# Second attention: the column of x with the key bias as a row sum on VectorE and ScalarE, instead of one-column products on TensorE

## The reference

```python
q = jnp.einsum('bld,de->ble', query_states, Wq) + bq
k = jnp.einsum('bld,de->ble', key_states, Wk) + bk
v = jnp.einsum('bld,de->ble', value_states, Wv) + bv
scores = jnp.einsum('bqd,bkd->bqk', q, k) / math.sqrt(HEAD_SIZE)
scores = scores + (1.0 - attention_mask)[:, None, :] * -10000.0
probs = jax.nn.softmax(scores, axis=-1)
context = jnp.einsum('bqk,bkd->bqd', probs, v)
```

## Time and profile before

| | us |
|---|---|
| median of 3 runs (377.69 to 378.69) | 377.79 |
| profiled execution, its own time | 375.65 |
| span of its instructions | 373.9 |
| TensorE busy | 354.1 |
| VectorE busy | 182.5 |
| ScalarE busy | 149.7 |
| GpSimd busy | 57.6 |

### The profile page before, as it was taken

One profiled execution on the slowest core, in us unless ns is written; L12 is line 12 of the kernel. 1 busy time (PEld: TensorE's weight loads), 2 busy tenths in 40 slices (PEclk: granted clock), 3 DMA queues, 4 the chain that ended last, 5 costly groups with the idle time before them and its releaser, 6 DMA issues.

```text
span 373.9 us, 7935 instructions
## 1 busy us (share of the span) xinstructions
PE 354.1 (95%) x3108; PEld 266.4 (71%) x3108; DVE 182.5 (49%) x573; ACT 149.7 (40%) x361; POOL 57.6 (15%) x95
## 2 busy tenths in 40 slices
PE   3889999999999999998889999999889999999996
PEld 2446666766657665755668998998768889797875
DVE  4964345647566465564462122212489667532500
ACT  0524553554454553535533221120345667523300
POOL 2730000010101000010120000030694421200000
PEclk9999999999999999999999999999999999999999
DMA  8946060603400100000207499970110011111000
GB/s 245 351 111 227 0 225 3 220 20 96 144 1 15 28 4 13 2 15 2 70 12 213 136 334 335 303 210 25 50 50 1 3 53 52 40 39 50 26 25 25
DMA packets 24885, 35.29 MB, mean 94 GB/s; under 512 B 2608, under 2 KB 21408, under 8 KB 24736
## 3 DMA queue, kind: packets, MB, share of 16 engines
q1 hardware_dynamic: 22160, 31.73, 26.9%
q0 software_dynamic: 768, 1.84, 1.7%
q10 hardware_dynamic: 1920, 1.21, 1.2%
HBM read 31.06 MB, written 3.72 MB: 93 GB/s over the span
## 4 chain that ended last, share of the span: by engine, by line
PE 85%; DVE 6%; DMA 5%; issue 2%; ACT 1%; POOL 0%; SPq 0%; DVEq 0%; ACTq 0%; POOLq 0%
PE ps L417 10%; PE ps L575 8%; PE ps L720 8%; PE ps L585 7%; PE ps L431 7%; PE ps L698 6%; PE ps L454 6%; PE ps L385 6%; PE ps L361 5%; PE ps L651 3%; PE ps L352 3%; DMA xres<-in_x 2%; PE ps L667 2%; PE ps L477 2%; PE ps L521 2%
## 5 line engine op out<-in xcount | busy, mean ns | idle before, releaser
L1056 DVE TENSOR_REDUCE mneg<-ps 112x2 f32<-112x750 f32 x64 | 57.1, 933 | 42.3 <-PE ps L417 41.9
L833 ACT ACTIVATE heads<-ps 125x896 f32<-125x896 f32 x48 | 41.4, 915 | 17.5 <-PE ps L437 17.5
L1273 POOL TENSOR_TENSOR rstd<-veps,neghalf 112x1 f32<-112x1 f32 x32 | 18.5, 577 | 194.1 <-DVE veps L1022 193.9
L417 PE MATMUL ps<-heads 32*112 32x375 f32 x256 | 38.5, 518 | 1.8 <-DVE mneg L1056 1.4
L431 PE MATMUL ps<-heads 32*125 32x224 f32 x384 | 32.2, 374 | 0.7 <-DVE mneg L1056 0.6
L361 PE MATMUL ps<-ctxT,w_in 128*128 128x375 f32 x64 | 25.6, 524 | 7.3 <-DMA ctxT<-in_ctxT 5.9
L575 PEld LDWEIGHTS ps<-xT,ring 128*128 128x128 f32 x256 | 29.8, 192 | 1.1 <-ACT xT L788 0.7
L575 PE MATMUL ps<-xT,ring 128*128 128x112 f32 x256 | 29.9, 275 | 0.4 <-ACT xT L788 0.4
L720 PE MATMUL ps<-heads,ring 128*112 128x256 f32 x128 | 28.8, 382 | 0.0
L585 PE MATMUL ps<-ring,heads 128*112 128x256 f32 x128 | 28.8, 379 | 0.0
L454 PEld LDWEIGHTS ps<-heads,vones 125*17 125x17 f32 x768 | 17.2, 97 | 13.9 <-issue 12.6
(11 more groups left out here) (140 smaller groups left out, 523.3 us busy)
## 6 DMA issues: line engine op xcount, KB each, us to landing
ring<-in_L_ffn_W SPq DMA_DIRECT2D x16, 1024.0 KB, 6.7
ctxT<-in_ctxT SPq DMA_DIRECT2D x8, 375.0 KB, 11.0
heads<-in_L_ffn_W SPq DMA_DIRECT2D x2, 1024.0 KB, 10.4
ring<-x_by_odd_rows_dram SPq DMA_DIRECT2D x4, 448.0 KB, 3.6
ring<-in_mask SPq DMA_DIRECT2D x1, 1312.5 KB, 7.4
expert_in_dram<-eo SPq DMA_DIRECT2D x1, 896.0 KB, 11.2
b2row<-in_L_ffn_b SPq DMA_DIRECT2D x8, 112.0 KB, 7.6
out_dram<-ring SPq DMA_DIRECT2D x8, 112.0 KB, 1.9
```

The lines of the kernel that those rows point to most:

```text
L417: mm = pe.matmul(bank(j)[0:S, 0:S2], qz[rows, m, a, b * S:(b + 1) * S], kt[b % 3][rows, m, :], start=True, stop=True)
L833: act.activation(pT[w % 2][0:KC, pair.start:pair.stop, :], ps[0:KC, pair.start:pair.stop, 0:2 * QW], ACT.Exp, scale=DK ** -0.5).then_inc(f ...
L1056: v.tensor_reduce(mneg[:, b % 2, PAIRS * g + pair.start:PAIRS * g + pair.stop], ps[0:S, pair.start:pair.stop, 0:S2], AX.X, ALU.max, negate ...
```

## The change

The term x (Wq bk) + bq·bk of each row is no longer made by TensorE. The fold now computes Wq bk as a row, repeated over 112 partitions: `bk_wide` (bk spread over 112 columns) times Wq, 256 columns wide. ScalarE copies it to `row_bias` and divides bq·bk by 256. For each batch VectorE multiplies the normalised rows by `row_bias` (`by_row_bias`), and ScalarE adds bq·bk/256 to each element and sums over the row into `tq`. Two semaphores are new: `by_row_ready` (VectorE to ScalarE) and `tq_ready` (ScalarE to VectorE). The buffers `row_bias` and `by_row` are cut ahead of the later ones in the same region, which move by them.

```diff
@@ fold, TensorE @@
-            pe.wait_ge(bq_ready, 1)
+            pe.wait_ge(bk_ready, 1)
             o = open_bank("WQKB", 1)
-            for side in range(2):
-                for m in range(DT):
-                    for k in range(DT):
-                        pe.matmul(o[:, DT * side + m:DT * side + m + 1], w_at1[:, 1 - side, k, m * P:(m + 1) * P],
-                                  bcol[:, 2 + side, k:k + 1], start=k == 0, stop=k == DT - 1)
+            for m in range(DT):
+                for k in range(DT):
+                    pe.matmul(o[:, D + m:D + m + 1], w_at1[:, 1, k, m * P:(m + 1) * P], bcol[:, 2, k:k + 1],
+                              start=k == 0, stop=k == DT - 1)
             for k in range(DT):
-                mm = pe.matmul(o[0:S, 2 * DT:2 * DT + 1], bq_wide[:, k, :], bcol[:, 3, k:k + 1],
-                               start=k == 0, stop=k == DT - 1)
+                pe.matmul(o[0:S, D + DT:D + DT + 1], bk_wide[:, k, :], bcol[:, 2, k:k + 1],
+                          start=k == 0, stop=k == DT - 1)
+            for k in range(DT):
+                mm = pe.matmul(o[0:S, 0:D], bk_wide[:, k, :], w_at1[:, 0, k, :], start=k == 0, stop=k == DT - 1)
             mm.then_inc(filled[1], 1)
@@ stage 1, TensorE @@
-                    for k in range(DT):
-                        mm = pe.matmul(o[0:S, 2 * S:2 * S + 1], xT[:, k, b * S:(b + 1) * S],
-                                       qk_bias[:, DT + k:DT + k + 1], start=k == 0, stop=k == DT - 1)
                     mm.then_inc(filled[1], 1)
@@ stage 1, ScalarE @@
                     o, free = full(("QK", b))
-                    act.activation(tq[s][0:S, :], o[0:S, 2 * S:2 * S + 1], ACT.Identity, bias=bqbk[0:S, :])
                     for m in range(DT):
                         ins = act.activation(qkT[s][:, m, :], o[:, m * S:(m + 1) * S], ACT.Identity,
                                              bias=qk_bias[:, m:m + 1])
                     ins.then_inc(free, 1)
+                    act.wait_ge(by_row_ready, b + 1)
+                    act.activation(by_row[s][0:S, :], by_row[s][0:S, :], ACT.Identity, bias=bqbk[0:S, :],
+                                   accum_out=tq[s][0:S, :]).then_inc(tq_ready, 1)
@@ fold, ScalarE @@
-            act.activation(qk_bias[:, :], o[:, 0:2 * DT], ACT.Copy)
-            act.activation(bqbk[0:S, :], o[0:S, 2 * DT:2 * DT + 1], ACT.Copy).then_inc(free, 1)
+            act.activation(qk_bias[:, :], o[:, D:D + DT], ACT.Copy)
+
+            act.activation(bqbk[0:S, :], o[0:S, D + DT:D + DT + 1], ACT.Copy, scale=1.0 / D)
+            act.activation(row_bias[0:S, :], o[0:S, 0:D], ACT.Copy).then_inc(free, 1)
@@ stage 2, VectorE @@
                     v.wait_ge(mask_ready, b + 1)
+                    v.wait_ge(tq_ready, b + 1)
@@ VectorE, new @@
+            def by_row_bias(b):
+
+                if b == 0:
+                    drained_by_me("WQKB")
+                if b >= 2:
+                    v.wait_ge(tq_ready, b - 1)
+                v.wait_ge(xn_ready, ROWS_DONE[3, b])
+                v.tensor_tensor(by_row[b % 2][0:S, :], xn[:, b, :], row_bias[0:S, :], ALU.mult)\
+                 .then_inc(by_row_ready, 1)
@@ VectorE, the loop @@
                 if i < NB:
                     normalise(3, i)
+                    by_row_bias(i)
                 for b in combined_in(i):
                     combine(b)
```

More of the change, by code:

```diff
@@ L183, in build @@
         w_at1 = cut(heads, 2 * DT * D).rearrange("p (w k e) -> p w k e", w=2, k=DT)
-        bq_wide = cut(heads, DT * S).rearrange("p (k s) -> p k s", k=DT)
+        bk_wide = cut(heads, DT * S).rearrange("p (k s) -> p k s", k=DT)
         w1f = cut(heads, DT * F).rearrange("p (k f) -> p k f", k=DT)
@@ L229, in build @@
         wqk = cut(late, DT * D).rearrange("p (k e) -> p k e", k=DT)
-        qk_bias = cut(late, 2 * DT)
+        qk_bias = cut(late, DT)
         bqbk = cut(late, 1)
@@ L239, in build @@
         pT1 = [cut(late, NKC * S).rearrange("p (c s) -> p c s", c=NKC) for _ in range(2)]
+        row_bias = cut(late, D)
+        by_row = [cut(late, D) for _ in range(2)]
         sm1 = cut(late, 4 * NB).rearrange("p (b j) -> p b j", j=4)
@@ L302, in build @@
         got_rows = [sem(f"rows_got{b}") for b in range(NB)]
-        bq_ready = sem("bq_wide_ready")
+        bk_ready = sem("bk_wide_ready")
+        by_row_ready = sem("rows_by_bias_ready")
+        tq_ready = sem("row_terms_ready")
         mask_ready = sem("mask_terms_ready")
@@ L640, in attend @@
                         for k in range(DT):
-                            pe.matmul(o[:, m * S:(m + 1) * S], wqk[:, k, m * P:(m + 1) * P],
-                                      xT[:, k, b * S:(b + 1) * S], start=k == 0, stop=k == DT - 1)
-                    for k in range(DT):
-                        mm = pe.matmul(o[0:S, 2 * S:2 * S + 1], xT[:, k, b * S:(b + 1) * S],
-                                       qk_bias[:, DT + k:DT + k + 1], start=k == 0, stop=k == DT - 1)
+                            mm = pe.matmul(o[:, m * S:(m + 1) * S], wqk[:, k, m * P:(m + 1) * P],
+                                           xT[:, k, b * S:(b + 1) * S], start=k == 0, stop=k == DT - 1)
                     mm.then_inc(filled[1], 1)
@@ L1141, in _ @@
             v.wait_ge(*filled_at(("ST", NB - 1, SCORE_STEPS - 1, HIGH)))
-            v.tensor_copy(bq_wide[:, :, :], bcol[:, 2, :].unsqueeze(2).broadcast_to([P, DT, S]))\
-             .then_inc(bq_ready, 1)
+            v.tensor_copy(bk_wide[:, :, :], bcol[:, 3, :].unsqueeze(2).broadcast_to([P, DT, S]))\
+             .then_inc(bk_ready, 1)
             v.wait_ge(pv_units, SCORE_STEPS * NB)
```

## The result

The changed kernel is slower: 380.82 us against 378.25 (medians of 7 runs each), ratio 1.0079, 95% interval 1.0053 to 1.0106. The difference of the medians is 2.57 us; the ratio, which is not simply theirs, makes 3.0. Run again in another comparison it gave 1.0103 (1.0061 to 1.0144). The prediction had 377.6 us, in a range of 376.1 to 378.9, and no change that a measurement can tell.

What follows compares the result with a forecast made beforehand. TensorE was taken as the bound, with VectorE nearly full. TensorE's 1.9 us gain less a 1.8 us wait left 0.1 us: execution 375.5 us, plus 2.14 to the median, rounded to 377.6; range 376.1 to 378.9.

Steps and rivals of the forecast that it cites:

- The fold: Computing Wq bk as a row: 0.1 us more on TensorE, about 0.4 on ScalarE, hidden under a wait; priced at nothing.
- The start: Batch 1's scores: VectorE's first product comes 0.45 us later, cancelling TensorE's 0.48 saving, so they start as before.
- In iteration 4: VectorE's five products cost 2.25 us, idle and overlap absorb some; batch 2's scores 1.2 us late, TensorE waits about 1.8.
- The product's price: VectorE's added product per batch: 0.33 us of queue plus 0.12 waiting for the normalisation, together 0.45; bounds 0.32 and 0.60.
- The collisions: VectorE against GpSimd's addition: one block of 0.46 us as before, with the product meeting it in the combine's place.
- After iteration 4: VectorE's iteration 3.9 us, TensorE's 4.2: TensorE bounds again, batches 4 to 7 return 1.28 us, ending 0.1 earlier.
- the third rival: VectorE's products and GpSimd's additions block each other, VectorE's iteration 4.35 us: 378.6 us; slower by this or another rival 0.13.
- the second form: Blocking rival with a second collision ahead of batch 2's scores: 379.1 us; slower by blocking or another rival 0.13.
- The row sum: ScalarE's sum over 256 columns, between 0.3 and 0.59 us, ready before VectorE needs it; priced at nothing.
- a sign of being wrong: In the changed profile, ScalarE's row sum releasing VectorE's instruction on the scores would show the prediction wrong.

Runs made afterwards that it cites:

- e1: The changed kernel without the row term: VectorE's product, ScalarE's row sum and their waits left out; ratio 0.9937 to the kernel before.
- e9: The changed kernel with VectorE's wait for the row term of batch b - 2 placed ahead of the normalisation; ratio 1.0045 to the kernel before.
- e6: The changed kernel with batch 0's product with the values put in bank 7 instead of bank 6; ratio 1.0081 to the kernel before.
- e5: The kernel before, one-column products kept, with a dead VectorE product of two SBUF tiles added per batch; ratio 1.0059 to the kernel before.
- e10: The kernel before with e5's dead products and a second, long-passed wait ahead of them for batches 4 to 7; ratio 1.0100 to the kernel before.
- e7: The changed kernel without GpSimd's eight additions of the value bias and the wait for them; ratio 1.0013 to the kernel before.

## Why the prediction was wrong, step by step

**Right.** The fold cost nothing: TensorE's first transpose came 270.90 - 262.18 = 8.72 us after the experts' addition, before 8.75. The start cancelled: the scores of batch 1 began 17.00 us after it, before 16.96. TensorE's queue held some 2 us of one-column products (e1: 2.4 by the ratios and 1.40 in the stretch, with a wait of 0.66 left), and without them its iteration is 4.15 us (e9), predicted 4.2. VectorE's delay became a wait of TensorE; in the change it stood at the bank (1.46 us), and only in e6 at the transpose of batch 2.

**Luck.** The wait in e6 was 1.81 us, predicted 1.8, but both parts of that sum were wrong. The prediction had VectorE 1.2 us late and TensorE there 0.64 early, at 285.83 for 286.47. In e6 VectorE was 2.2 late, and TensorE was there 27.20 us after the experts' addition (288.80 - 261.60), 0.25 later than before's 26.95, having waited for ScalarE at the scores of batch 1 and the transpose of batch 0 (0.50 and 0.52).

**The step that failed: "In iteration 4 ... 2.25 - 0.50 - 0.36 - 0.2 = 1.2 us", so that L1188 of batch 2 would be 1.2 us late.** Measured by the experts' addition it is 290.42 - 262.18 = 28.24 against 285.50 - 259.52 = 25.98: 2.26 late. Two terms were mis-sized.
- *The product's price.* From the normalisation's start to the next combine it is 0.86 us (270.43 to 271.29) against 0.32, so 0.54 and not 0.45: its start behind the end of the normalisation took 0.11 us, not 0.03. The five products come to 2.94 us in that way, batch 3's at 0.87 since it met an addition.
- *The collisions.* I had kept the one collision of before and added none. The combines of batches 3 and 4 took 0.52 and 0.51 us more, and in exchange the 0.94 of before did not come. 2.94 + 1.03 - 0.46 - 0.30 (the long L1026) - 0.50 - 0.36 = 2.35, measured 2.26. TensorE's transpose began 0.79 us behind the end of L1195 (290.42 to 291.21), not 0.97, and so is 2.08 late.

**The second step that failed: "After iteration 4 ... TensorE is the bound again, nothing more is lost", 1.28 us returned.** As good as nothing was: the transpose of batch 2 is 2.08 us late, that of batch 5 2.02. L1195 comes at 290.27, 294.86, 299.45: VectorE's iteration is 4.59 us, not 3.9, and it stays the bound. The difference is the block of 0.56 at each product, its later start (0.07), and L1191, which now has one more semaphore and starts 0.18 us behind L1028, where before it was 0.11. I had priced this as the third rival (VectorE's iteration 4.35) and argued it away with "the product follows on its own queue 0.03 behind the normalisation, GpSimd 0.08 behind it". The 0.08 was right (291.07 to 291.15), the 0.03 holds for one semaphore only; this product waits for two from batch 2 on and starts 0.10 behind (291.07 to 291.17). e9, e5 and e10 show that this decides it. The Trainium skill, "SBUF — State Buffer", section "Who interferes with whom", has the rule: the later of the two is blocked. At the products these rows agree, both ways round (0.99 us for the product that began second, 0.97 for the addition that did); at the combine of batch 3 the recorded starts do not, see the end.

The rival's mechanism was the right one and its price too small: 0.8 us above before (378.6), or 1.3 with a second collision ahead of batch 2's scores (379.1, outside the range given), against 2.6. Ahead of those scores collisions added 0.52, 0.51 and 0.33 us and took away the 0.46 of before, so the second form was the nearer one. Both forms had the cheaper product, and both let TensorE's saving come back in iterations 5 to 7, less 0.15 each.

**The row sum: "Price nothing".** It takes 0.51 us with 0.20 for its sum, and no run shows that it costs anything. The profile puts one wait of VectorE down to it (0.38 us at 303.17, ahead of batch 5's scores), and the prediction had named such a wait as a sign of being wrong. But the row term of batch 5 was made at 297.86; the L930 that ended just before 303.17 is batch 6's. And e9 has the same 0.38 us ahead of the same instruction with nothing named (e7 0.37). What VectorE waited for there stays open.

**The last 0.57 us.** From the transpose of batch 5 (43.15 after, 41.13 before) to that of batch 6 (48.04, 45.45) the change loses another 0.57 us. Batch 5's exponential is late behind VectorE (idle 1.53 at 304.58). The copies for the last layer stand behind it in ScalarE's queue, and L942 behind those, for which TensorE waited 0.54 us at 307.57. The prediction had "TensorE is the bound again" here too. The timeline after, VectorE, ScalarE and who waits:

```profile
297.86 0.51 ACT L930 ACTIVATE ring<-ring 112x256 f32<-112x256 f32 x1
...
302.45 0.51 ACT L930 ACTIVATE ring<-ring 112x256 f32<-112x256 f32 x1
...
303.17 0.61 DVE L1191 SCALAR_TENSOR_TENSOR ring<-ps,ring 112x375 f32<-112x375 f32 x1 [0.38 <-ACT ring L930]
...
304.58 0.61 ACT L936 ACTIVATE ring<-ring 112x375 f32<-112x375 f32 x1 [1.53 <-DVE ring L1195]
...
305.43 0.69 ACT L961 ACTIVATE ring<-ps,scale_t 4x112 f32<-4x112 f32 x2
306.14 0.36 ACT L790 ACTIVATE xT<-ps 128x224 f32<-128x224 f32 x1
...
306.52 0.67 ACT L949 ACTIVATE ring<-xn 32x256 f32<-32x256 f32 x1
307.09 0.42 ACT L942 ACTIVATE ring<-ps 125x336 f32<-125x336 f32 x1
...
307.57 1.55 PE L669 MATMUL ps<-ctxV,ring 125*112 125x256 f32 x6 [0.54 <-ACT ring L942]
```

And the same place in e9:

```profile
301.42 0.61 DVE L1191 SCALAR_TENSOR_TENSOR ring<-ps,ring 112x375 f32<-112x375 f32 x1 [0.38 <-issue]
```

In e9, with the same row sum but VectorE in time, the transposes of batches 5 and 6 stand at 42.21 and 46.17, 3.96 apart: the row sum alone does not make this loss, and neither do the 0.38 us, which e9 has too. It takes the late VectorE besides; how the loss is shared among them is not shown.

## What to carry to other kernels

Work moved off the bound engine is paid for on the engine that receives it, and at 5.68 of 6.10 us busy that engine had 0.4 us an iteration to give, not 0.54 and its collisions. Before moving a term, ask whether the result needs it: here softmax cancels it. When an instruction with two inputs in SBUF is put where another queue's instruction is released by the same event, ask which of the two starts first and make it the one that matters, by waiting for all else beforehand or by keeping one input in PSUM. A wait found in the trace is worth removing only if the next wait hangs on something else; here two waits hung on one queue.

## What the runs showed of the hardware that was not expected

- A VectorE product behind one semaphore wait started 0.03 us after the instruction that it waited for (e9, e5), behind two waits 0.10 us (the change, e10).
- Whoever of VectorE's product and GpSimd's addition started first, by 0.02 to 0.05 us, kept its length; the other grew: the product from 0.43 to 0.99 us, the addition from 0.73 to 0.97.
- The order of recorded starts does not explain every case. The combine of batch 3 is recorded 0.07 us ahead of the inverse root in the change (274.60 and 274.67) and in e7 (276.12 and 276.19); it took 1.00 us in the first, where the addition follows the root, and 0.48 in the second, where none does. Why the addition, recorded 0.62 us later, can lengthen it was not settled.
- A blocked instruction did not lose the whole overlap: the product in the change ended 0.28 us after the addition (292.16 and 291.88), though it takes 0.43 alone; the addition in e9 ended 0.59 us after the product (292.24 and 291.65), though it takes 0.73.
- Profiled executions differ by several us ahead of the changed work (259.52 to 265.19 us to the experts' last addition), and in these 14 traces they stand in order of their number of 3.4 us spells at the lower granted clock: none, one, two, three. A prediction made against a single execution has to be read from a common point behind that.
